# The three row gathers at the end of GpSimd's step in place of its front

## The reference, cut to what matters

```
x = x + (x @ weight[b] + bias[b])        # weight[b] = U[b] @ V, rank 30, decoded from cond_512
h = LN(x) * pw_g[path] + pw_b[path]      # a table row of each token, 500 rows
h = LN(h) * cp_g[comp] + cp_b[comp]      # 5 rows
t = LN(x) * tm_g[comp] + tm_b[comp]      # 5 rows
s = LN(x) * ms_g[scale] + ms_b[scale]    # 3 rows
m, n, r = x + a row of each batch        # from three small networks
cat = [w0 h, w1 t, w2 m, w3 n, w4 r, w5 s]
x = x + LN(silu(cat @ int_W1 + b1) @ int_W2 + b2) * int_g + int_be
```

## Time and profile before

| | |
|---|---|
| median of 3 runs | 667.28 us (666.37 to 667.55) |
| the profiled execution | 665.57 us |
| its span, first to last instruction | 663.7 us |
| TensorE busy | 593.9 us, 89% |
| VectorE busy | 456.4 us, 69% |
| GpSimd busy | 383.4 us, 58% |
| ScalarE busy | 157.1 us, 24% |
| gathers' queue (q0) | 42.04 MB, 19.6% of 16 DMA engines' span |
| SyncE's queue (q1) | 58.52 MB, 25.8% |
| mean granted TensorE clock | 0.977 of full speed |

### The profile page before, as it was taken

How to read it: one execution, slowest core, us unless ns; L and a number is a source line. 1 busy time by engine, 2 the same in 40 slices (tenths; PEclk the granted TensorE clock), 3 DMA queues, 4 the chain that set the end, 5 groups by cost and what they waited for, 6 DMA issues and landing times.

```text
span 663.7 us, 9039 instructions
## 1 busy us (share of the span) xinstructions
PE 593.9 (89%) x2912; PEld 457.5 (69%) x2912; DVE 456.4 (69%) x808; ACT 157.1 (24%) x278; POOL 383.4 (58%) x438
## 2 busy tenths in 40 slices
PE   0897887977999999998899999999999999999982
PEld 0454454455777777777778888888888888888861
DVE  3410277467887888888887787877787878777731
ACT  3332242231222222222222222222222222222110
POOL 1022333555777776677777767677676767666410
PEclk9999798989999999999999999999999999999996
DMA  8999961523434443444434444443444433343000
GB/s 296 404 403 376 387 244 62 173 90 131 131 131 131 131 132 130 131 134 140 143 108 132 132 131 130 130 130 130 130 130 130 130 130 130 130 130 112 17 31 16
DMA packets 52968, 101.99 MB, mean 154 GB/s; under 512 B 10430, under 2 KB 22974, under 8 KB 52812
## 3 DMA queue, kind: packets, MB, share of 16 engines
q1 hardware_dynamic: 39728, 58.52, 25.8%
q0 software_dynamic: 12160, 42.04, 19.6%
q10 hardware_dynamic: 1052, 1.07, 0.5%
HBM read 93.10 MB, written 8.39 MB: 153 GB/s over the span
## 4 chain that ended last, share of the span: by engine, by line
PE 59%; DVE 12%; POOL 11%; issue 10%; DMA 4%; SPq 1%; ACT 1%; POOLq 0%; DVEq 0%; ACTq 0%
PE bank L634 16%; PE bank L635 15%; PE bank L636 15%; PE bank L628 5%; DMA ring<-in_W_dec 4%; POOL rs L892 3%; DVE bn L1094 3%; POOL xb L938 2%; POOL ve L888 2%; DVE st L1145 2%; POOL ctt L911 2%; PE bank L622 2%; DVE ops L1089 2%; POOL sgt L911 2%; PE bank L685 1%
## 5 line engine op out<-in xcount | busy, mean ns | idle before, releaser
L634 PE MATMUL bank<-W,ops 128*128 128x512 f32 x432 | 178.2, 412 | 6.5 <-DVE ops L1089 6.5
L635 PE MATMUL bank<-W,ops 128*128 128x512 f32 x432 | 171.0, 396 | 0.0
L636 PE MATMUL bank<-W,ops 128*128 128x512 f32 x432 | 170.8, 395 | 0.0
L634 PEld LDWEIGHTS bank<-W,ops 128*128 128x128 f32 x432 | 82.8, 192 | 34.5 <-issue 14.8
L522 ACT ACTIVATE ops<-bank 128x512 fp32r<-128x512 f32 x96 | 53.9, 594 | 184.4 <-PE bank L628 184.4
L636 PEld LDWEIGHTS bank<-W,ops 128*128 128x128 f32 x432 | 82.4, 191 | 18.2
L635 PEld LDWEIGHTS bank<-W,ops 128*128 128x128 f32 x432 | 82.8, 192 | 14.6
L938 POOL TENSOR_TENSOR xb<-x,bebc 128x512 f32<-128x512 f32 x32 | 41.7, 1304 | 67.1 <-DVE y L1228 67.1
L1089 DVE TENSOR_TENSOR ops<-bank,ops 128x512 fp32r<-128x512 f32 x96 | 63.0, 683 | 17.6 <-ACT ops L522 17.6
L927 POOL TENSOR_TENSOR h<-xhat,pwt 128x512 f32<-128x512 f32 x32 | 57.6, 1800 | 22.1 <-DVE xhat L1132 22.1
L888 POOL TENSOR_SCALAR ve<-mv 128x1 f32<-128x1 f32 x96 | 30.5, 318 | 62.6 <-DVE mv L1098 58.3
(11 more groups left out here) (123 smaller groups left out, 1035.9 us busy)
## 6 DMA issues: line engine op xcount, KB each, us to landing
ring<-in_W_dec SPq DMA_DIRECT2D x16, 960.0 KB, 12.2
xraw<-in_xT SPq DMA_DIRECT2D x32, 256.0 KB
x<-in_x SPq DMA_DIRECT2D x32, 256.0 KB, 5.9
out<-y SPq DMA_DIRECT2D x32, 256.0 KB
ring<-in_int_W SPq DMA_DIRECT2D x4, 1024.0 KB, 13.6
mnr<-in_int_W SPq DMA_DIRECT2D x12, 256.0 KB, 8.3
stash<-in_xT SPq DMA_DIRECT2D x12, 256.0 KB, 11.8
idxrep<-in_rows SPq DMA_DIRECT2D x64, 32.0 KB, 5.4
```

What stands on the lines that cost most here:

```text
L634: nc.tensor.matmul(bank[:, :], op[:, HI, c, :], w[:, HI, c, :], start=start and c == 0, stop=False)
L635: nc.tensor.matmul(bank[:, :], op[:, HI, c, :], w[:, LO, c, :], start=False, stop=False)
L636: last = nc.tensor.matmul(bank[:, :], op[:, LO, c, :], w[:, HI, c, :], start=False, stop=stop and c == KC - 1)
```

## The change

In GpSimd's step the call of `gathers(a)` moves from the front to behind the third `rstd`, just ahead of `residual(f)`. `first_step` keeps its own order.

```diff
 def step(n):
     a, f, c = n.plus(2), n.plus(1), n.plus(-1)
-    if a.exists():
-        gathers(a)
     if f.exists():
         rstd(0, f, mv1_ready, r1_ready)
         h_first(f)
...
     if c.exists():
         rstd(2, c, mv3_ready, r3_ready)
+    if a.exists():
+        gathers(a)
     if f.exists():
         residual(f)
```

## The result

| | before | after |
|---|---|---|
| median | 667.41 us (666.37 to 667.73, 4 runs) | 683.46 us (682.06 to 687.53, 4 runs) |
| ratio | | 1.0262, 95% interval 1.0229 to 1.0295 |
| the profiled execution / its span | 665.57 / 663.7 us | 687.53 / 685.7 us |
| step of the first stage, last rs to last rs, mean of 10 | 15.93 us | 17.05 us |
| step of the second stage, mean of 16 | 16.71 us | 17.36 us |

The kernel became 16.0 us slower, where I had forecast 4.3 us and a range that ended at 678.5. The direction was right, the size and the range were wrong. The prologue won 1.9 us (last rs of step 1 at 151.58 against 153.47 us), and step 2 lost them again (168.81 against 168.84).

What follows compares the result with a forecast made beforehand. VectorE and GpSimd in turn were taken to bound the first stage, TensorE the second. Landing +6.2 us, prologue -1.9, the rest 0 made +4.3 us: 671.5 us against a median of 667.28, range 663.5 to 678.5.

Steps and rivals of the forecast that it cites:

- (a): Front of a first-stage step: without gathers there, rs waits for mv alone; 0.84 us a step saved, period 15.1 us.
- (b): VectorE's CAST and OH beside GpSimd's xb, now after the gathers: put at 0, between -0.4 and +0.7 us.
- (c): Prologue's end, step 1: tile 2's rs no longer behind tile 3's gathers; 1.9 us gained once, between 1.5 and 2.5.
- (d): First stage: h waits for pwt's late landing, closing a new circle; period 16.5 us, +0.56 a step, +6.2 in 11 steps.
- L: Time from issue to landing of pwt's gather, taken as 6.6 us; the first-stage period was to be 9.9 + L.
- (e): Second stage: pwt lands in 5.2 to 6.1 us, within TensorE's 16.8 us step; cost 0, at most 2 us in all.
- (f): SyncE: idx and idxrep loads come up to 6 us later but are needed a whole step later; cost 0.

Runs made afterwards that it cites:

- split_gathers: Kernel before, with pwt's gather left at the front of GpSimd's step and only ctt's and sgt's moved to its end; 664.73 us, ratio 0.9973.
- stage1_only: Kernel before, with the gathers moved to the end of GpSimd's step in steps 1 to 13 only; 673.58 us, ratio 1.0116.
- pw_first: Changed kernel, with the three gathers at the step's end issued in the order pwt, ctt, sgt; 675.06 us, ratio 1.0123 to the kernel before.
- fence: Changed kernel, with a 128x1 memset and a wait for it between the last gather and xb; 671.14 us, ratio 1.0063 to the kernel before.
- step1_only: Kernel before, with the gathers moved to the end of GpSimd's step in step 1 alone; 664.31 us, ratio 0.9965.
- stage2_only: Kernel before, with the gathers moved to the end of GpSimd's step from step 14 on only; 671.96 us, ratio 1.0074.
- act_swap: Changed kernel, with ScalarE making the high half of h ahead of the high half of x; 676.85 us, ratio 1.0141 to the kernel before.
- fence_act_swap: Changed kernel, with a memset and wait between last gather and xb, and ScalarE's high half of h ahead of x's; 665.74 us, ratio 0.9986 to before.
- act_swap_on_before: Kernel before, with only ScalarE's high half of h put ahead of the high half of x; 666.01 us, ratio 0.9994.

## Why the prediction was wrong in size

- *(a), the front of the step:* the mechanism was right (xhat waits 0.46 us for rs in place of 1.28), and in after it gained nothing, since mv came later by more. Where the landing is out of the way (split_gathers) it is worth 0.53 us a step; there CAST takes 0.83 us in place of 0.62 and mv comes 0.28 us later (6.58 for 6.30), which is nearly all of the rest to 15.1. A slip in the sum: I counted 0.98 us from mv to rs where my own two terms make 1.02; after has 1.00 (193.83 to 194.83).
- *(b), CAST, OH and xb: the step that failed in the first stage.* I put it at 0, "between -0.4 and +0.7 us". CAST did fall to 0.23 us, as bounded. But I let xb hold VectorE only while it runs, and looked at OH; the held one is stack's second instruction, ahead of OH in the circle, and the hold begins during the gather: +1.50 us (1.85 for 0.35), less 0.39 for CAST, is 1.11, and mv came 1.15 us later (7.47 for 6.32). With (a)'s 15.1 that makes 16.2, about the 16.3 of stage1_only's later steps and of seven steps of pw_first. The runs bracket it: with the fence the first stage falls by 1.28 us a step, some 14 us over 11 steps. The bound from below was sound, the one from above took the wrong victim and too short a hold. The Trainium skill (SBUF — State Buffer, Who interferes with whom) was cited there with its rule that whoever issues first blocks the other for a whole instruction; the rows agree only in kind, since by the profile's start times stack began first (189.68 us, xb 190.10) and was the one held. That the hold reaches back over the gather in front of xb is shown by fence against after, 0.28 against 1.84 us.
- *The late stack also costs clock,* which I didn't foresee. Where TensorE idled 2.58 and 2.42 us at it, the expand matmul took 0.80 us, and the granted clock was 0.51 for the next 3 us; where it idled 1.5 us it took 0.51 and the clock stayed. In fence it idled at most 1.03 us and the clock stayed at 1.00. The length of this one wait does not settle it: in pw_first the clock stayed at 1.00 once after 2.63 us (at 275.08). The two kinds of step tell landing and clock apart. In after, steps 4, 6, 8, 10 and 12 have a mean clock of 0.90 and take 17.21 to 17.26 us, nearly 1.0 above 16.3, though pwt is in time or nearly so; steps 3, 5, 7, 9 and 11 have 1.00 and h late, and take 16.48 to 17.22, 0.6 above it in the mean. Over the ten steps that is 0.5 us a step beside the lower clock and 0.3 beside the late landing, together the 0.75 between 16.3 and 17.05. That is a reading by kind of step, not an experiment: each kind may bring on the other.
- *(c), the prologue:* the mechanism was right: xhat at 133.51 (forecast 133.8), offset products at 138.91 us (139.2). The sum took the 1.9 us as kept to the end; in after they are gone at the last rs of step 2. That step1_only's median also gained 1.9 us is in part luck, since its profiled execution too has lost the lead by then.
- *(d), the landing circle:* the median landing was 6.7 us (forecast 6.6), so L was well read. The circle was 0.5 to 0.8 us shorter than 9.9 + L: 2.78 + 6.32 = 9.1 in the step shown, since the two passes of a late h are shorter (1.50 and 1.28 us, against 1.80 and 1.62) and the output's statistics are ready by then. With the hold cured, the first stage is that circle: fence has L = 6.4 and 15.77 us a step, where 9.9 + L says 16.3. By this term the change comes out about even in the first stage (15.77 against 15.93, where I had +0.56); the loss that I forecast came from elsewhere.
- *(e), the second stage at 0: the other step that failed.* I asked only whether pwt would be in time. The landing of xraw, issued behind the gathers, wasn't priced: 6.3 us at the median, and ScalarE waits for it ahead of h's high half. The stage costs 5.9 us by itself (stage2_only). Nor did pwt keep to the 5.2 to 6.1 us that I gave it: it landed after 5.8 to 7.9, and h waited 28 us in 11 of 14 steps. Either cure is enough here: pw_first (pwt early) takes 16.81 us a step and act_swap (ScalarE's order turned) 16.77. My 5 us between ctt and xraw and this landing both came true in act_swap (4.8 us, and 5.5 us at the median), where TensorE set the pace; in after it did not. The row that could have told was the order on ScalarE, x before h, together with the wait for xraw that was there already.
- *(f), SyncE:* no run shows a loss from idx or idxrep coming late; nothing waits for them in the waits that were read.

So the sign of +4.3 was right by luck, for a reason that explains little of the loss: the hold with the clock that follows it, and the late xraw and pwt of the second stage, make nearly all of the 16 us. (The upper end of my range is slightly off too: 667.28 + 12 is about 679, not 678.5; it changes nothing.) fence_act_swap, which cures both stages, is within 0.2% of the kernel before.

## What to carry to other kernels

When a DMA issue of GpSimd is moved, look at what stands right behind it: here xb, with nothing to wait for, held VectorE from early in the issue to its own end. A wait in between (a tiny memset and its semaphore) put xb off by 0.2 us here and gave back 1.3 a step. When transfers are moved, price not only when they land themselves but every load that is now issued behind them, and read the order on the engine that receives it: a late input does harm through what stands behind it in that order. Of a group of transfers, move each for itself: pwt was needed at once and ctt and sgt were not, and the split, with ScalarE's order turned, was worth 1.3% where the whole move cost 2.6%.

## What the runs showed of the hardware that was not expected

- VectorE was held over 1.85 us for a 32x128 instruction that needs 0.28, from some point in the gather's issue to xb's end. CAST, begun 0.28 us into the issue (189.42 against 189.14), ran freely in 0.23; stack, 0.54 us into it, was held. The point can be read from all traces in which xb stands right behind a gather. Of CAST, stack's second instruction and OH, none begun later than 0.31 us into the issue ran freely, and none begun earlier than 0.28 us was held (75 were held, up to 2.14 us long in pw_first). VectorE's instructions with a bank among their operands (inner, z, x1) and the statistics of x ran freely wherever they began, up to 0.91 us into the issue. In the three kernels with the fence none of the first three kinds, begun during a gather's issue, was held. In the second stage OH was held likewise, here 0.35 us into the issue of 480.86 and until xb's end at 483.11 (VectorE, after):

```profile
480.89 0.29 DVE L1112 TENSOR_TENSOR stack<-inner,stack 32x128 fp32r<-32x128 f32 x1
481.21 2.00 DVE L1055 TENSOR_SCALAR OH<-idxrep,cst 128x128 fp32r<-128x128 int32 x1
```

- The landing went with the place among the three gathers, for either tile: pwt issued last landed after 6.1 to 8.0 us (after, first stage), issued first after 4.3 to 5.3 us (pw_first); ctt issued first after 4.1 to 5.2 us (after), issued second after 6.4 to 7.6 us (pw_first).
- The order on ScalarE was worth nothing while xraw came in time (act_swap_on_before, 0.9994) and 1.2% in the changed kernel, and it moved the landings themselves: xraw from 6.3 to 4.0 us and pwt from 7.3 to 5.5 us at the median (second stage of after and of act_swap).
